# Softmax sums inverted in a compact layout, shared semaphores for emptied banks, and new numbers in the kernel's own planner

## The chip, the cores and the metric

One core of one Trainium2 chip runs the whole program. The time is device microseconds (us) for one execution. The core has five instruction streams: PE (TensorE, matmuls into PSUM), DVE (VectorE), ACT (ScalarE), POOL (GpSimd) and SP (SyncE, which here only issues DMAs). Each stream runs its instructions in the order in which they were written, and waits in front of an instruction until the semaphores it names have reached their values.

## The reference, cut to what matters

The input x is 4 batches of 1024 rows of 256 numbers in fp32. Three blocks follow one another, each with a residual:

```
x = x + 0.5 * ffn(layernorm(x))        # gate and up 256->704, silu(g) * u, down 704->256
x = x + attention(layernorm(x))        # 16 heads of 16, rotary positions, causal softmax
x = x + 0.5 * ffn(layernorm(x))        # the same weights again
```

The attention scores of a head are q.k / 4 with a causal mask; the softmax subtracts the maximum of the row, takes the exponential, and divides by the sum of the row. It is this division that the change touches.

## The kernel before, in words

**Stages.** The first feed-forward block works on 8 chunks of 512 rows (`ffn`, `x_pass`). Attention follows in 16 groups: 4 batches, and in each 4 groups of 4 heads (`NG = 4`, `GROUPS = 16`). The second feed-forward block is again 8 chunks. Products are formed from high and low parts in a rounded 32-bit format, so most matmuls come in threes.

**One group of attention** has two sweeps. The first (`maxima`, L861 and L871) computes the scores with queries on the partitions (piece `pe_s`), and DVE takes the maximum of each row from PSUM (`dve_max`, L1148). The maxima are gathered by DVE (`dve_nm`, L1157 to L1164), transposed by PE (L878), copied by ACT (L1015) and sent through a DRAM buffer (`nw`, L1343, and `nm`, L1350) into two extra rows of Q. The second sweep (`heads`) computes the scores transposed, shift included (`pe_st`, L892); ACT takes the exponential out of PSUM (`act_exp`, L1029); POOL zeroes the half above the diagonal (`pool_mask`, L1252); and PE multiplies with V (`pe_pv`, L909). V has 17 columns per head, the last one all ones, so row 17 of a head's result is the sum of its softmax. The first sweep of group n+1 runs beside the second sweep of group n. The projections for q, k and v of the next batch (L773) are laid between.

**The division.** For each group and each half of 512 queries (`c2`), ACT copies the result from PSUM to `OS` (`act_o`, L1037), SP writes it to DRAM (`ow`, L1356) and reads it back twice (`oc`): the 16 value rows of each head into `OC` (L1368), and the sum row broadcast to the same 16 partitions into `SC` (L1369). When two groups have filled the 128 partitions, DVE takes the reciprocal of the whole 128x512 tile `SC` in place (`dve_rc`, L1170), POOL multiplies (`pool_on`, L1258), ACT and POOL split the product into a high and a low part (L1042, L1263), and PE projects it (`pe_o`).

**The planner.** No order of work is written out by hand. `timetable()` lists all pieces with a place (a due time in us), a cost in ns, the pieces they come after, and the PSUM banks they need. `settle()` then plays the five streams forward: on an engine other than PE it takes the ready piece with the smallest place; on PE it takes the ready piece with the smallest cost-adjusted place that finds free banks and lies within `WINDOW` of the first piece not yet begun. `LAG` is the time that it adds from the end of a piece to its being visible elsewhere, `QUOTA` how many of the 8 banks the pieces `pe_s` and `pe_st` may hold, `MODE_PLACE` and `MODE_NS` what a change of matmul shape costs, `DMA_RATE` bytes per ns. The order and the banks that come out are what the streams are written from, so a wrong number in the planner costs no correctness, only a different order.

**Semaphores.** Each kind of piece has a semaphore of its own. Before a matmul writes into a bank, `take` waits for the pieces that emptied it. `wait_ge` leaves out a wait for a value that this engine has already met on the same semaphore.

The division in `heads`, as the planner sees it: `dve_rc` has the place `key + 6` and the cost `dve_ns(512)`, which is 65 + 512 / 0.96 = 598 ns.

Of the kernel before, what the change touches and what calls it, by code (L numbers as in the profile page):

```python
# [75 lines left out]

INNER = {"dve_va": ("dve_bn", "dve_ag"), "dve_nm": ("dve_mn", "dve_nh"), "pool_r": ("pool_ts", "pool_tc"), "dve_flagint": ("dve_flagsum",)}
# [31 lines left out]
LAG = {"PE": 165, "ACT": 130, "DVE": 90, "POOL": 80, "SP": 1900}  # L109
# [15 lines left out]
class Timetable:  # L125
# [21 lines left out]
    def settle(self):  # L147
# [30 lines left out]
        def choose(e):  # L178
# [23 lines left out]
        while todo or ends:  # L202
# [10 lines left out]
            for e in self.order:  # L213
                while free[e] <= now:
# [5 lines left out]
                    if e == "PE":  # L220
# [34 lines left out]
MODE_PLACE, MODE_NS, DMA_RATE, WINDOW = 2.0, 110, 250.0, 40.0  # L255
AHEAD = 4.0
QUOTA = {"pe_s": 4, "pe_st": 4}
# [37 lines left out]
def timetable():  # L295
# [18 lines left out]
    def x_pass(who, c, at):  # L314
# [7 lines left out]
        add(at + 2, 4 * 290, "act_xn", who, c, after=[("dve_nb", who, c)] + ([("pe_xT",) + xn + (1,)] if xn else []))  # L322
        for kt in range(2):
            add(at + 4, 436, "pe_xT", who, c, kt, after=[("act_xn", who, c), ("act_id",)] + (x_users(*x) if x else []), room=(1,))
# [26 lines left out]
    def ffn(ph, c, at):  # L351
        who, last = f"f{ph}", []
        for i in range(NI):
# [9 lines left out]
            if i < NI - 1:  # L363
                add(key, 908, "pe_g", ph, c, i, after=x_in(who, c) + w + room, room=(1,))
            add(key + 1, 908, "pe_u", ph, c, i, after=x_in(who, c) + w + room, room=(1,))
            gate = ("pe_g" if i < NI - 1 else "pe_u", ph, c, i)
            add(key + 1, act_ns(512) + 90, "act_silu", ph, c, i, after=[gate] + ([("dve_h",) + g] if g else []) + first,
# [3 lines left out]
            add(key + 2, act_ns(512), "act_hh", ph, c, i, after=[("dve_h", ph, c, i)] + room)  # L371
# [19 lines left out]
    def qkv(b, cc, at, z):  # L391
# [4 lines left out]
        for w in range(2):  # L396
            p.ring("T", 1, (b, cc, w))
            was = p.prior["T", (b, cc, w)]
            for ab in range(2):
                add(key(2 * w + ab), 1362, "pe_qk", b, cc, w, ab, after=x_in("a", c) + [("act_wh", "q"), ("pool_wl", "q")] + ([("pool_zl",) + was] if was else split), room=(1,))  # L400
# [30 lines left out]
    def maxima(gr, at, z):  # L431
# [3 lines left out]
        for c2 in range(2):  # L435
            drained = []
            for unit, n in zip(units, cost):
# [7 lines left out]
                add(key, mask + (2 if u == "a" else 1) * (wide * 0.443 + 12), "pe_s", *unit, after=[ld(gr, ch), ld(gr, c2), ("act_mk",)],  # L445
# [15 lines left out]
    def heads(gr, at, z):  # L461
# [4 lines left out]
        for unit, n in zip(units, cost):  # L466
# [5 lines left out]
            add(key, (2 if u == "a" else 1) * (max(512 - skip, 256) * 0.443 + 12), "pe_st", *unit,  # L472
# [6 lines left out]
            if u != 0:  # L479
# [6 lines left out]
                else:  # L486
                    w = sum({0: 1000, 128: 780, 256: 590, 384: 460}[e_skip(c2, i)] for i in (j - 1, j)) - 150
# [4 lines left out]
            if (j, u) == (4 * c2 + 3, "a"):  # L492
# [61 lines left out]
class Engine:  # L554
# [13 lines left out]
def macaron(nc, x_in, wgu, wd, wqkv, wo, gsc, usc, dsc, ident_in, cos_in, sin_in, mask_in, out):  # L568
    ctx = ExitStack()
    with ctx:  # L570
# [11 lines left out]
        def lay(at, *items):  # L582

            made = []
            for name, shape, dt in items:
# [15 lines left out]
        NH = place("NH", [P, 4])  # L601
        ONE = place("ONE", [P, 1])
        FL = place("FL", [P, 16])
        FS = place("FS", [1, 1])
        FLAG = place("FLAG", [1, 2], I32)
        ST, MV, VE, RS, NB = ([place(f"{n}{i}", [P, 4] + s) for i in range(2)]
                              for n, s in (("ST", [6]), ("MV", [2]), ("VE", []), ("RS", []), ("NB", [])))
        NP = [place(f"NP{i}", [P, 2, BT, 4]) for i in range(2)]
        NM = [place(f"NM{i}", [P, 2, 2, 2, 2, 4], F32R) for i in range(2)]
        NMT = [place(f"NMT{i}", [32, P], F32R) for i in range(2)]  # L610
        ONES = place("ONES", [2, 32], F32R)
# [55 lines left out]
        OD = nc.dram_tensor("od", (2, P, 512), F32, kind="Internal").ap()  # L667
        WGD = nc.dram_tensor("wgd", (2, P, 2, GUW), F32, kind="Internal").ap()
# [13 lines left out]
        for name in ("PE", "ACT", "DVE", "POOL", "SP"):  # L682
            for piece in plan.order[name]:
                for sem, by in raises(piece):
# [3 lines left out]
                    done[(sem,) + piece[1:]] = count[sem]  # L688
        pe, act, dve, pool, sp = (Engine(n, sems, done) for n in ("PE", "ACT", "DVE", "POOL", "SP"))
        S = sems  # L690
# [71 lines left out]
        def tensor_program(e, todo, general):  # L762
            tn = nc.tensor

            def take(piece):

                for was in emptied.get(piece, ()):
# [8 lines left out]
            for piece in todo:  # L776
# [24 lines left out]
                elif kind == "pe_flag":  # L801
# [3 lines left out]
                    tn.matmul(bank(*piece)[0:1, 0:6], ONE[:, 0:1], FL[:, 8:14], start=True, stop=True).then_inc(S["pe_flag"], 1)  # L805
# [238 lines left out]
        def vector_program(e):  # L1044
            ve = nc.vector
            for piece in plan.order["DVE"]:
                kind, a = piece[0], piece[1:]
                if kind == "dve_va":
# [15 lines left out]
                    ve.tensor_scalar(VE[k][:, :], MV[k][:, :, 1], EPS, None, ALU.add).then_inc(S["dve_va"], 1)  # L1064
                elif kind == "dve_nb":
# [3 lines left out]
                    ve.scalar_tensor_tensor(NB[k][:, :], MV[k][:, :, 0], -1.0, RS[k][:, :], ALU.mult, ALU.mult).then_inc(S["dve_nb"], 1)  # L1069
# [14 lines left out]
                elif kind == "dve_flagint":  # L1084
                    e.wait_ge("pe_flag")
                    ve.tensor_reduce(out=FS[0:1, 0:1], in_=bank("pe_flag")[0:1, 0:6], axis=AX, op=ALU.add).then_inc(S["dve_flagsum"], 1)
# [387 lines left out]
```

## Time and profile before

| | us |
|---|---|
| median of 3 runs | 982.24 |
| lowest and highest of the 3 | 974.79 and 982.36 |
| the profiled execution | 987.35 |
| its span, first to last instruction | 985.6 |

The profile is of one execution. Busy times are those of an engine's instructions; waits, branches and the issue of DMAs are not counted as busy. A PE weight load (PEld) overlaps the matmuls. The mean granted TensorE clock of the execution is 0.908 of full speed. Full speed is 2.4 GHz and the lower level, 0.50, is 1.2 GHz.

### The profile page before, as it was taken

How to read it: one execution, taken by the hardware profiler on the slowest of the kernel's cores; microseconds unless marked ns; L12 is line 12 of the kernel's file. 1: busy time of each engine (PE TensorE's matmuls, PEld its weight loads, DVE VectorE, ACT ScalarE, POOL GpSimd, SP SyncE). 2: the span in 40 equal slices, each digit the busy share in tenths (PEclk: the TensorE clock that was granted, in tenths of full speed). 3: DMA queues.
4: the chain of work that ended last, by engine and by line, in shares of the span. 5: the costliest groups of instructions: out<-in, count | busy, mean ns of one | idle time of the engine just before them, and what ended most of it. 6: DMA issues, size and time to landing. Idle time of an engine off the chain costs nothing.

```text
span 985.6 us, 17031 instructions
## 1 busy us (share of the span) xinstructions
PE 861.6 (87%) x6064; PEld 545.0 (55%) x6064; DVE 682.0 (69%) x1257; ACT 563.2 (57%) x1102; POOL 386.1 (39%) x361
## 2 busy tenths in 40 slices
PE   5699999969988989988898998798978878899996
PEld 4477888745544445644444464344434334777785
DVE  5575675868988779877787878777786742655442
ACT  5555665437465656664665655465635686465652
POOL 6556776352432234333134143221121322565453
PEclk9799999979996989986897988788979898999999
DMA  9500333035553325245054233431830110000101
GB/s 320 227 1 1 123 102 97 2 68 155 156 168 86 77 98 137 76 138 145 31 144 103 103 103 136 107 79 37 269 101 34 45 34 23 26 28 22 44 23 43
DMA packets 52320, 91.44 MB, mean 93 GB/s; under 512 B 6028, under 2 KB 17676, under 8 KB 51724
## 3 DMA queue, kind: packets, MB, share of 16 engines
q1 hardware_dynamic: 52092, 90.27, 30.2%
q8 instruction: 51, 0.84, 0.4%
q14 instruction: 33, 0.27, 0.1%
q10 hardware_dynamic: 144, 0.07, 0.0%
HBM read 47.49 MB, written 42.73 MB: 92 GB/s over the span
## 4 chain that ended last, share of the span: by engine, by line
PE 60%; DVE 15%; ACT 14%; issue 5%; DMA 2%; POOL 2%; SPq 1%; DVEq 0%; POOLq 0%; ACTq 0%
PE psum L909 12%; PE psum L799 12%; PE psum L773 10%; PE psum L861 9%; PE psum L892 7%; PE psum L824 7%; DVE NP L1148 7%; ACT PT L1029 5%; DVE SC L1170 3%; ACT XN L958 3%; PE psum L871 2%; ACT G_f L977 2%; DMA SC<-od 1%; ACT HH_f L987 1%; ACT XH L965 1%
## 5 line engine op out<-in xcount | busy, mean ns | idle before, releaser
L1148 DVE TENSOR_REDUCE NP<-psum 128x1 f32<-128x512 f32 (+3 forms) x640 | 364.3, 628 | 104.0 <-PE psum L871 74.3
L1029 ACT ACTIVATE PT<-psum 128x512 f32<-128x512 f32 (+2 forms) x640 | 307.9, 568 | 180.6 <-PE psum L892 179.5
L861 PE MATMUL psum<-K,Q 48*128 48x512 f32 (+2 forms) x768 | 159.8, 441 | 41.8 <-DVE NP L1148 31.7
L892 PE MATMUL psum<-Q,K 50*128 50x512 f32 (+2 forms) x768 | 153.8, 443 | 33.1 <-ACT PT L1029 18.0
L909 PE MATMUL psum<-PT,V 128*32 128x512 f32 (+3 forms) x1536 | 170.3, 568 | 0.4 <-ACT PT L1029 0.4
L1252 POOL TENSOR_SCALAR_AFFINE_SELECT PT<-PT 128x512 f32<-128x512 f32 x128 | 80.8, 638 | 206.1 <-ACT PT L1029 205.8
L799 PE MATMUL psum<-XH,WGH_f 128*128 128x512 f32 x352 | 147.2, 418 | 15.4 <-issue 6.7
L861 PEld LDWEIGHTS psum<-K,Q 48*128 48x128 f32 x768 | 77.1, 204 | 125.8 <-DVE NP L1148 48.5
L799 PE MATMUL psum<-XL,WGH_f 128*128 128x512 f32 x352 | 141.0, 401 | 0.0
L1209 POOL TENSOR_TENSOR HL_f<-HF_f,HH_f 128x512 fp32r<-128x512 f32 x80 | 103.0, 1294 | 94.1 <-ACT HH_f L987 93.8
L892 PEld LDWEIGHTS psum<-Q,K 50*128 50x128 f32 x768 | 77.4, 210 | 80.1 <-ACT PT L1029 31.8
L1099 DVE SCALAR_TENSOR_TENSOR HF_f<-psum,US,G_f 128x512 f32<-128x512 f32 x96 | 71.6, 750 | 58.8 <-ACT G_f L977 28.6
L824 PE MATMUL psum<-WDH_f,HH_f 128*128 128x256 f32 x384 | 90.0, 287 | 6.4 <-DVE HH_f L1106 5.6
L987 ACT ACTIVATE HH_f<-HF_f 128x512 fp32r<-128x512 f32 x96 | 60.4, 629 | 59.8 <-DVE HF_f L1099 59.0
L977 ACT ACTIVATE G_f<-psum,GS 128x512 f32<-128x512 f32 x96 | 64.8, 681 | 45.9 <-PE psum L799 45.1
L799 PEld LDWEIGHTS psum<-XH,WGH_f 128*128 128x128 f32 x352 | 67.8, 193 | 41.1 <-ACT G_f L977 9.3
L909 PEld LDWEIGHTS psum<-PT,V 128*32 128x32 f32 x1536 | 43.5, 118 | 78.7 <-issue 56.8
L824 PE MATMUL psum<-WDH_f,HL_f 128*128 128x256 f32 x320 | 78.9, 283 | 0.0
L824 PEld LDWEIGHTS psum<-WDH_f,HH_f 128*128 128x128 f32 x384 | 71.3, 193 | 11.4 <-issue 6.7
L799 PEld LDWEIGHTS psum<-XL,WGH_f 128*128 128x128 f32 x352 | 67.9, 193 | 12.8
L1258 POOL TENSOR_TENSOR OC<-OC,SC 128x512 f32<-128x512 f32 x16 | 20.3, 1270 | 131.5 <-DVE SC L1170 131.5
L824 PEld LDWEIGHTS psum<-WDH_f,HL_f 128*128 128x128 f32 x320 | 61.6, 192 | 0.4
(81 smaller groups left out, 1087.2 us busy)
## 6 DMA issues: line engine op xcount, KB each, us to landing
zd<-ZH SPq DMA_DIRECT2D x32, 512.0 KB, 3.8
Q<-zd SPq DMA_DIRECT2D x64, 192.0 KB, 3.7
K<-zd SPq DMA_DIRECT2D x64, 192.0 KB, 4.5
zd<-ZL SPq DMA_DIRECT2D x16, 512.0 KB, 4.6
od<-OS SPq DMA_DIRECT2D x32, 256.0 KB, 2.8
OC<-od SPq DMA_DIRECT2D x32, 128.0 KB
SC<-od SPq DMA_DIRECT2D x32, 128.0 KB
out<-X SPq DMA_DIRECT2D x16, 256.0 KB, 2.1
```

Of the source, the lines that this page charges most:

```text
L773: ins = tn.matmul(dst, x, w, start=(m == 0), stop=(m == len(terms) - 1))
L799: ins = tn.matmul(bank(*piece), w[ph][:, kt, col:col + P], x[k][:, kt, :], start=(n == 1), stop=(n == 6))
L824: ins = tn.matmul(dst, h[:, rows], w[ph][:, i, :], start=(n == 0), stop=(n == len(terms) - 1))
L861: ins = tn.matmul(dst, Q[k][r, p, t * P:(t + 1) * P], K[k][r, p, ch * 512:ch * 512 + w], start=(m == 0), stop=not diag)
L892: ins = tn.matmul(dst, K[k][r, p, j * P:(j + 1) * P], Q[k][r, p, 512 * c2 + base:512 * c2 + 512], start=True, stop=True)
L909: ins = tn.matmul(bank(*piece)[32 * h:32 * h + 32, skip:512], V[b % 2][:, col:col + 32], pt_view(gr, c2, j)[:, h, :], start=(j == 0), stop ...
L977: sc.activation(G[ph][slot[f"Gf{ph}", a]][ul, :], bank(*gate)[gl, :], ACT.Silu, scale=GS[gl, i:i + 1]).then_inc(S["act_silu"], 1)
L1029: sc.activation(dst, src, ACT.Exp, scale=0.25).then_inc(S["act_exp"], 1)
L1099: ve.scalar_tensor_tensor(HF[ph][k][ul, :], bank("pe_u", *a)[ul, :], US[ul, i:i + 1], G[ph][k][ul, :], ALU.mult, ALU.mult).then_inc(S["dve ...
L1148: ve.tensor_reduce(out=acc, in_=src, axis=AX, op=ALU.max, negate=True).then_inc(S["dve_max"], 1)
L1209: gp_.tensor_tensor(HL[ph][s][:, :], HF[ph][slot[f"Gf{ph}", a]][:, :], f32(HH[ph][s][:, :]), ALU.subtract).then_inc(S["pool_hl"], 1)
L1252: gp_.affine_select(out=pt, in_=pt, compare_op=ALU.is_ge, fill=0.0, base=0, pattern=[[0, 4], [1, P]], channel_multiplier=-1).then_inc(S["p ...
```

## The change

It has three parts.

1. **Division.** A new DMA `rs` reads the 4 x 512 sums of a group and half from DRAM into a compact tile `SU` of 128 partitions by 16; DVE takes the reciprocal of that tile into `RC`, once per group and half (32 times in place of 16); a new DMA `rw` writes it to a DRAM buffer `rd_`. The second read of `oc` now broadcasts the inverted sums from there. `pool_on` waits for the two `oc` of its groups and no longer for DVE.
2. **Semaphores.** The pieces of ACT that can empty a bank share one semaphore, `act_out`, and those of DVE another, `dve_out`. `take` goes through the emptying pieces from the highest value down, so that one wait per engine is left.
3. **The planner's numbers.** Lags, costs of pieces, the price of a change of shape and of a wait for two engines, a larger window (60 for 40), a quota of 5 banks for 4, and an urgency `URGE` by which `pe_s` and `pe_st` go ahead of other PE work while they hold few banks.

The small tiles of the layer norm are also placed differently in memory, with the same instructions on them.

```diff
-LAG = {"PE": 165, "ACT": 130, "DVE": 90, "POOL": 80, "SP": 1900}
+LAG = {"PE": 200, "ACT": 190, "DVE": 150, "POOL": 120, "SP": 1900}
...
-                cost = item[0] + (0 if self.mode[item[2]] == mode[0] else MODE_PLACE)
+                kind = item[2][0]
+                cost = item[0] + (0 if self.mode[item[2]] == mode[0] else MODE_PLACE) - URGE.get(kind, (0,) * 9)[held.get(kind, 0)]
...
-                            ns += MODE_NS
+                            ns += MODE_NS[mode[0], self.mode[piece]]
                             mode[0] = self.mode[piece]
+                        ns += WAIT_NS * (len({engine[x] for x in self.emptied.get(piece, ())}) - 1 > 0)
...
-MODE_PLACE, MODE_NS, DMA_RATE, WINDOW = 2.0, 110, 250.0, 40.0
+MODE_PLACE, WAIT_NS, DMA_RATE, WINDOW = 1.0, 80, 200.0, 60.0
+MODE_NS = {("full", "half"): 190, ("col", "half"): 110, ("half", "full"): 30, ("half", "col"): 30, ("full", "col"): 60, ("col", "full"): 60}
-QUOTA = {"pe_s": 4, "pe_st": 4}
+URGE = {"pe_s": (12, 12, 12, 12, 4, 0, 0), "pe_st": (12, 12, 8, 8, 0, 0, 0)}
+QUOTA = {"pe_s": 5, "pe_st": 5}
...
-                add(key, mask + (2 if u == "a" else 1) * (wide * 0.443 + 12), "pe_s", *unit, ...
+                add(key, mask + (2 if u == "a" else 1) * (wide * 0.443 + 40), "pe_s", *unit, ...
...
-                    w = sum({0: 1000, 128: 780, 256: 590, 384: 460}[e_skip(c2, i)] for i in (j - 1, j)) - 150
+                    w = sum({0: 790, 128: 600, 256: 420, 384: 250}[e_skip(c2, i)] for i in (j - 1, j))
...
+                add(key + 2.6, 600, *turn_of("rs", gr, c2), after=[turn_of("ow", gr, c2)])
+                add(key + 2.6, 280, "dve_rc", gr, c2, after=[turn_of("rs", gr, c2)] + ([turn_of("rw", *was)] if gr else []))
+                add(key + 2.6, 600, *turn_of("rw", gr, c2), after=[("dve_rc", gr, c2)] + ([turn_of("oc", *was)] if gr else []))
-                add(key + 2.5, 1200, *turn_of("oc", gr, c2), after=[turn_of("ow", gr, c2)] + free, size=2.6e5)
+                add(key + 2.6, 1200, *turn_of("oc", gr, c2), after=[turn_of("ow", gr, c2), turn_of("rw", gr, c2)] + free, size=2.6e5)
...
-                    add(key + 6, dve_ns(512), "dve_rc", b, gp, c2, after=[turn_of("oc", gr - 1, c2), turn_of("oc", gr, c2)])
-                    add(key + 6, pool_ns(512), "pool_on", b, gp, c2, after=[("dve_rc", b, gp, c2)])
+                    add(key + 6, pool_ns(512), "pool_on", b, gp, c2, after=[turn_of("oc", gr - 1, c2), turn_of("oc", gr, c2)])
...
     def wait_ge(self, sem, *step):
         value = self.done[(sem,) + step]
+        sem = EMPTIES.get(sem, sem)
...
-                for was in emptied.get(piece, ()):
+                for was in sorted(emptied.get(piece, ()), key=lambda was: -done[was]):
                     e.wait_ge(*was)
...
                 elif kind == "dve_rc":
-                    b, gp, c2 = a
-                    for g in range(2):
-                        e.wait_ge(*turn_of("oc", NG * b + 2 * gp + g, c2))
-                    n = 2 * (2 * gp + c2)
-                    ve.reciprocal(OC[n + 1][:, :], OC[n + 1][:, :]).then_inc(S["dve_rc"], 1)
+                    gr, c2 = a
+                    e.wait_ge(*turn_of("rs", gr, c2))
+                    if gr:
+                        e.wait_ge(*turn_of("rw", gr - 1, c2))
+                    ve.reciprocal(RC[c2][:, :], SU[c2][:, :]).then_inc(S["dve_rc"], 1)
...
+                elif name[:2] == "rs":
+                    gr, c2 = a
+                    e.wait_ge(*turn_of("ow", gr, c2))
+                    if gr:
+                        e.wait_ge("dve_rc", gr - 1, c2)
+                    src = OD[c2].rearrange("(h r) q -> h r q", h=4)[:, HD, :].rearrange("h (a n) -> h a n", n=16)
+                    sy.dma_start(SU[c2][:, :], src).then_inc(sem, 16)
+                elif name[:2] == "rw":
+                    gr, c2 = a
+                    e.wait_ge("dve_rc", gr, c2)
+                    if gr:
+                        e.wait_ge(*turn_of("oc", gr - 1, c2))
+                    sy.dma_start(RD_[c2].rearrange("h (a n) -> h a n", n=16), RC[c2][:, :]).then_inc(sem, 16)
...
-                    sy.dma_start(sc_[r, :], src[:, HD:HD + 1, :].broadcast_to([4, HD, 512])).then_inc(sem, 16)
+                    sy.dma_start(sc_[r, :], RD_[c2].unsqueeze(1).broadcast_to([4, HD, 512])).then_inc(sem, 16)
```

Other costs of pieces that change: the transposes of x 436 to 400 ns, the four normalising activations 1160 to 1964, gate and up 908 to 925, silu 567 to 586, the high part of the hidden tile 477 to 550, q and k projections 1362 to 1385.

## Rows read from the trace of the kernel before

**Rows 1.** The page, parts 1 and 2: busy time of each engine, and the granted clock.
```profile
PE 861.6 (87%) x6064; PEld 545.0 (55%) x6064; DVE 682.0 (69%) x1257; ACT 563.2 (57%) x1102; POOL 386.1 (39%) x361
PEclk9799999979996989986897988788979898999999
```

**Rows 2.** Windows by stage: length, busy of five engines, granted clock, DMA share, GB/s.
```profile
0.00:208.00 208.00, 179.33 (x1014) 145.06 (x1014) 137.50 (x290) 112.31 (x189) 121.30 (x96) 0.98 0.30 104
225.00:808.00 583.00, 514.89 (x4084) 271.24 (x4084) 457.44 (x815) 348.80 (x736) 168.51 (x186) 0.87 0.37 106
```

**Rows 3.** The chain that ended last: by line; first and last of ten stretches.
```profile
PE psum L909 12%; PE psum L799 12%; PE psum L773 10%; PE psum L861 9%; PE psum L892 7%; PE psum L824 7%; DVE NP L1148 7%; ACT PT L1029 5%; DVE SC L1170 3%; ACT XN L958 3%; PE psum L871 2%; ACT G_f L977 2%; DMA SC<-od 1%; ACT HH_f L987 1%; ACT XH L965 1%
...
312.53 3.26 DVE SC L1170
...
781.37 3.36 DVE SC L1170
```

**Rows 4.** Groups of instructions by line: busy, mean ns of one | idle before, releaser.
```profile
L1148 DVE TENSOR_REDUCE NP<-psum 128x1 f32<-128x512 f32 (+3 forms) x640 | 364.3, 628 | 104.0 <-PE psum L871 74.3
...
L1170 DVE RECIPROCAL SC<-SC 128x512 f32<-128x512 f32 x16 | 53.5, 3346 | 7.4 <-DMA SC<-od 7.4
...
L1162 DVE CAST NM<-NP 128x16 fp32r<-128x16 f32 x32 | 10.1, 316 | 1.0 <-DVE NP L1148 0.5
```

**Rows 5.** Timeline around one reciprocal: start, length, instruction, [idle before <-releaser].
```profile
357.06 3.35 DVE L1170 RECIPROCAL SC<-SC 128x512 f32<-128x512 f32 x1 [0.67 <-DMA SC<-od]
...
360.33 1.82 DVE L1148 TENSOR_REDUCE NP<-psum 128x1 f32<-128x512 f32 x3
...
361.60 0.80 PE L861 MATMUL psum<-K,Q 48*128 48x512 f32 x2 [3.20 <-DVE NP L1148]
```

**Rows 6.** Windows of 4 us, from 0.8 us after each of 16 reciprocals; one, and the sum.
```profile
357.90:361.90 4.00, 0.80 (x10) 0.29 (x2) 4.00 (x4) 0.11 (x1) 1.26 (x1) 0.82 0.97 358
...
sum 64.00, PE 29.20 PEld 13.94 DVE 61.38 ACT 24.82 POOL 27.20; mean PE 1.83 PEld 0.87 DVE 3.84 ACT 1.55 POOL 1.70
```

**Rows 7.** Windows of 14 us from the start of the 16 reciprocals: first, tenth, last.
```profile
289.10:303.10 14.00, 12.13 (x104) 6.68 (x105) 13.18 (x21) 9.04 (x21) 6.47 (x9) 0.73 0.88 234
...
636.00:650.00 14.00, 10.10 (x60) 4.14 (x60) 10.25 (x14) 6.68 (x14) 2.54 (x2) 0.60 0.05 20
...
842.00:856.00 14.00, 11.10 (x72) 9.42 (x71) 9.37 (x9) 6.02 (x10) 7.66 (x6) 1.00 0.01 1
```

**Rows 8.** Waits of PE in attention (225 to 808): total us, times, longest.
```profile
PE psum L861 <- DVE NP L1148: 31.7, 32, 3.6
PE psum L892 <- DVE NP L1148: 9.3, 8, 2.4
PE psum L892 <- ACT PT L1029: 9.1, 24, 0.9
...
PE psum L861 <- issue: 0.5, 2, 0.3
```

**Rows 9.** Waits around the division, whole span, and SP's longest wait.
```profile
POOL OC L1258 <- DVE SC L1170: 131.5, 16, 18.6
...
ACT OH L1042 <- POOL OC L1258: 32.3, 13, 4.3
...
DVE SC L1170 <- DMA SC<-od: 7.4, 5, 4.5
...
SPq L1343 <- ACT NMT L1015: 262.2, 28, 23.8
```

**Rows 10.** DMAs on the DRAM tensor of the division: issue and landing, min/median/max.
```profile
L1356 SPq DMA_DIRECT2D od<-OS x32: 319/344/1183, 227.5 to 834.4; - x32
...
DMA to landing us min/median/max: 2.0/2.8/15.3
```

**Rows 11.** The page, part 6: KB each, median us from issue to landing.
```profile
Q<-zd SPq DMA_DIRECT2D x64, 192.0 KB, 3.7
...
nmd<-NMT SPq DMA_DIRECT2D x32, 16.0 KB, 1.4
```

More of the change, by code:

```diff
@@ L363, in ffn @@
             if i < NI - 1:
-                add(key, 908, "pe_g", ph, c, i, after=x_in(who, c) + w + room, room=(1,))
-            add(key + 1, 908, "pe_u", ph, c, i, after=x_in(who, c) + w + room, room=(1,))
+                add(key, 925, "pe_g", ph, c, i, after=x_in(who, c) + w + room, room=(1,))
+            add(key + 1, 925, "pe_u", ph, c, i, after=x_in(who, c) + w + room, room=(1,))
             gate = ("pe_g" if i < NI - 1 else "pe_u", ph, c, i)
-            add(key + 1, act_ns(512) + 90, "act_silu", ph, c, i, after=[gate] + ([("dve_h",) + g] if g else []) + first,
+            add(key + 1, 586, "act_silu", ph, c, i, after=[gate] + ([("dve_h",) + g] if g else []) + first,
                 empties=[gate] if i < NI - 1 else [])
@@ L370, in ffn @@
                 empties=[("pe_u", ph, c, i)])
-            add(key + 2, act_ns(512), "act_hh", ph, c, i, after=[("dve_h", ph, c, i)] + room)
+            add(key + 2, 550, "act_hh", ph, c, i, after=[("dve_h", ph, c, i)] + room)
             add(key + 3, pool_ns(512) if i < NI - 1 else dve_ns(512), *hl_by(ph, c, i), after=[("act_hh", ph, c, i)])
@@ L399, in qkv @@
             for ab in range(2):
-                add(key(2 * w + ab), 1362, "pe_qk", b, cc, w, ab, after=x_in("a", c) + [("act_wh", "q"), ("pool_wl", "q")] + ([("pool_zl",) + was] if was else split), room=(1,))
+                add(key(2 * w + ab), 1385, "pe_qk", b, cc, w, ab, after=x_in("a", c) + [("act_wh", "q"), ("pool_wl", "q")] + ([("pool_zl",) + was] if was else split), room=(1,))
             banks_of = [("pe_qk", b, cc, w, ab) for ab in range(2)]
@@ L444, in maxima @@
                 mask = 0 if ch < c2 else (2 if u == "a" else 1) * 85
-                add(key, mask + (2 if u == "a" else 1) * (wide * 0.443 + 12), "pe_s", *unit, after=[ld(gr, ch), ld(gr, c2), ("act_mk",)],
+                add(key, mask + (2 if u == "a" else 1) * (wide * 0.443 + 40), "pe_s", *unit, after=[ld(gr, ch), ld(gr, c2), ("act_mk",)],
                     room=(2,), mode="half")
@@ L471, in heads @@
             was = pt_before(gr, c2, j)
-            add(key, (2 if u == "a" else 1) * (max(512 - skip, 256) * 0.443 + 12), "pe_st", *unit,
+            add(key, (2 if u == "a" else 1) * (max(512 - skip, 256) * 0.443 + 40), "pe_st", *unit,
                 after=([was] if was else ffn1_end) + [ld(gr, c2), ld(gr, j // 4), turn_of("nm", gr, c2), (f"dma_on{gr % QK}",)],
@@ L600, in macaron @@
         MB = place("MB", [P, P + 64], BF16)
-        NH = place("NH", [P, 4])
-        ONE = place("ONE", [P, 1])
+        CST = place("CST", [P, 8])
+        NH, ONE, FS = CST[:, 0:4], CST[:, 4:5], CST[0:1, 5:6]
         FL = place("FL", [P, 16])
-        FS = place("FS", [1, 1])
         FLAG = place("FLAG", [1, 2], I32)
-        ST, MV, VE, RS, NB = ([place(f"{n}{i}", [P, 4] + s) for i in range(2)]
-                              for n, s in (("ST", [6]), ("MV", [2]), ("VE", []), ("RS", []), ("NB", [])))
+        ST, MV = ([place(f"{n}{i}", [P, 4, s]) for i in range(2)] for n, s in (("ST", 6), ("MV", 2)))
+        ROW = place("ROW", [P, 2, 3, 4])
+        VE, RS, NB = ([ROW[:, i, n, :] for i in range(2)] for n in range(3))
         NP = [place(f"NP{i}", [P, 2, BT, 4]) for i in range(2)]
@@ L610, in macaron @@
         NMT = [place(f"NMT{i}", [32, P], F32R) for i in range(2)]
+        SU, RC = ([place(f"{n}{i}", [P, 16]) for i in range(2)] for n in ("SU", "RC"))
         ONES = place("ONES", [2, 32], F32R)
@@ L687, in macaron @@
                     count[sem] = count.get(sem, 0) + by
-                    done[(sem,) + piece[1:]] = count[sem]
+                    done[(signal,) + piece[1:]] = count[sem]
         pe, act, dve, pool, sp = (Engine(n, sems, done) for n in ("PE", "ACT", "DVE", "POOL", "SP"))
-        S = sems
+        S = sems | {signal: sems[sem] for signal, sem in EMPTIES.items() if sem in sems}
         def bank(*use):
@@ L804, in tensor_program @@
                     take(piece)
-                    tn.matmul(bank(*piece)[0:1, 0:6], ONE[:, 0:1], FL[:, 8:14], start=True, stop=True).then_inc(S["pe_flag"], 1)
+                    tn.matmul(bank(*piece)[0:1, 0:6], ONE, FL[:, 8:14], start=True, stop=True).then_inc(S["pe_flag"], 1)
                 elif kind == "pe_dn":
@@ L1085, in vector_program @@
                     e.wait_ge("pe_flag")
-                    ve.tensor_reduce(out=FS[0:1, 0:1], in_=bank("pe_flag")[0:1, 0:6], axis=AX, op=ALU.add).then_inc(S["dve_flagsum"], 1)
+                    ve.tensor_reduce(out=FS, in_=bank("pe_flag")[0:1, 0:6], axis=AX, op=ALU.add).then_inc(S["dve_flagsum"], 1)
                     e.wait_ge("dve_flagsum")
-                    ve.tensor_copy(FLAG[0:1, 0:1], FS[0:1, 0:1]).then_inc(S["dve_flagint"], 1)
+                    ve.tensor_copy(FLAG[0:1, 0:1], FS).then_inc(S["dve_flagint"], 1)
                 elif kind == "dve_h":
@@ L1255, in gpsimd_program @@
                     b, gp, c2 = a
-                    e.wait_ge("dve_rc", *a)
+                    for g in range(2):
+                        e.wait_ge(*turn_of("oc", NG * b + 2 * gp + g, c2))
                     n = 2 * (2 * gp + c2)
```

22 lines of the change are left out of this document (14 added, 8 removed).

## The prediction

> **What bounds the kernel now.** I read the page first. PE is busy 87% of the span and DVE 69%, and the row of granted clocks is full at both ends and ragged in the middle [rows 1]. The windows by stage say the same in numbers. The first feed-forward block runs at a clock of 0.98; attention, 225 to 808 us, takes 583 us at 0.87, with PE busy 514.9 us (88%) and DVE 457.4 us (78%) [rows 2]. So attention is where a change can gain. It has two losses. PE is idle for 583 - 514.9 = 68 us, and the clock below full costs 0.13 x 583 = 76 us, since PE at its lower level does half the work in the same busy time. PE's own waits there are on DVE emptying PSUM after the row maxima (31.7 + 9.3 us), and much less on ACT (9.1 us) [rows 8].
>
> DVE has long to do there (640 maxima of 628 ns), but one of its instructions is unlike the others: the reciprocal of a 128x512 tile, 16 times 3.35 us [rows 4]. The chain of waits that ended last goes through it ten times [rows 3]; the ten stretches add up to 31 us. The timeline around one shows how: DVE is shut for 3.35 us, no bank is emptied, and PE stands for 3.20 us until the maxima resume [rows 5]. The lower clock follows. In the 14 us from that start the clock is 0.76.
>
> **The change part by part.**
>
> *The old reciprocals go.* Take a window of 4 us from 0.8 us after each start, where PE has run out of banks: in the 16 windows PE is busy 29.2 of 64 us, 46% [rows 6]. At the 88% of the stage it would be 56.5 us. That is 27 us of PE time lost beside the 16 reciprocals, and I count it as regained. (The chain's 31 us is the same loss seen another way.)
>
> *The clock after them.* The 14 us from each start had clocks from 0.60 to 1.00 [rows 7], of which three stand there. For the 14 windows that lie in attention the mean is 0.74, a loss of 0.26 x 196 = 51 us of the stage's 76. The other 387 us of attention lose 25 us, 0.065 per us; at that rate the 196 us would have lost 13. So 38 us of clock loss goes with the reciprocals. Part of it has other causes close by (the window from 289 us is also one of heavy DMA traffic, 234 GB/s), and a PE that gets ahead meets its next wait sooner. I take half, 19 us; its bounds are 0 and 38.
>
> *The new reciprocals.* DVE has 32 on 128x16. The old instruction scaled by columns gives 3346 x 16 / 512 = 105 ns; the nearest row is another operation on 128x16, 316 ns [rows 4], and I take that: 32 x 0.316 = 10 us of DVE. What a us of DVE is worth comes from the old ones: (27 + 19) / 53.5 = 0.86. So -9 us (bounds -3 and -10).
>
> *The wait in front of them.* `dve_rc` now waits for `rs`, a DMA, which itself follows `ow`. Queued behind it on DVE are the row maxima, and for those PE waits. The old instruction waited 7.4 us in 16, its DMA having been due 3.5 us earlier than it (`key + 2.5` against `key + 6`) [rows 9]. At the same 0.46 us for each, 32 waits make 15 us; the old 7.4 go. Net 7.4 x 0.86 = -6 us. The lower bound is +6 (no waits left). The upper is the subject of a rival.
>
> *SP and the DMAs.* 64 DMAs more, about 8 KB each, with issues like the 344 ns of `od<-OS` [rows 10]: 22 us of SP's time in 583. SP spent 262 us in front of one line alone, waiting for ACT [rows 9], so it has room, and I cost it at nothing; without that room, `nm` and `ld` would come late by the round trip. The way from ACT's copy to `oc` grows by two hops. The small hop of the trace lands in 1.4 us and the loads of 192 KB in 3.7 [rows 11]; so 2 x (1.4 to 3.7) plus issue and reciprocal, 4 to 8 us, less the 3.35 that POOL's product no longer waits. It moves no end: PE has no row of waiting for the output projection, whose operands this is. The DMA traffic of attention fills 0.37 of the queues' time [rows 2]. The broadcast read is of the same size as before.
>
> The Trainium skill speaks against this part: "DMA: Bandwidth & Descriptors", in its rules for kernel authors, has it that transfers under 64 KB are mostly overhead, and its anatomy of one DMA gives a fixed cost of about 2 us, most of it the receipt of the write. By that, an estimate from that page of the skill, two hops add 4 us per group and half, 128 us in all, if each were waited out. The 16 KB row lands in 1.4 us, under the skill's figure, and nothing on PE waits for it, so I leave the sum as it is.
>
> *POOL and ACT behind the division.* POOL stood 131.5 us in front of `pool_on`, up to 18.6 us at once, and ACT 32.3 us in front of the high part that follows it [rows 9]. The planner booked the reciprocal at 598 ns where it took 3.35 us, so it placed both too early by 2.7 us: 12 x 2.7 = 32, which is ACT's row. With an honest cost they go. ACT has slack (349 of 583 us busy [rows 2]), so I count nothing here and keep it for the next term. Late next: `pool_on` behind the landing of `oc`, with the masks queued after it on POOL.
>
> *Semaphores.* They take waits out of PE's stream. The trace shows PE waiting for nothing but issue for 0.5 us in the whole stage [rows 8]. I take 0. From below it is 0, from above perhaps 5.
>
> *The new order.* What the planner will choose cannot be read off a trace. What it can win is bounded: 41 us of PE idling that is not beside reciprocals (68 - 27), 25 us of clock loss outside the windows and the 19 that I left inside: 85 us. The numbers move towards the rows (598 to 280 ns for a reciprocal that I put at 316). `URGE` and the fifth bank put the scores, which feed DVE and ACT, ahead of projections that nobody is in a hurry for, and DVE was idle for 104 us on the scores alone [rows 4]. Against it: fewer banks and later turns for `pe_pv`. I take about a fifth of the 85, 16 us, with -14 (the stage's 68 us of idling grow by a fifth) and 50 as ends. The feed-forward blocks I leave as they are: clock 0.98, and costs that moved by few per cent.
>
> **Sum.** 27 + 19 - 9 - 6 + 16 = 47 us. The profiled execution took 987.35 us (span 985.6), so it comes to 940 us. The median of the runs is 5 us under it, 982.24; I do not take off those 5, since three runs spread over 7.6 us. Forecast: **940 us**, 4.3% less than the median.
>
> **The rivals.** A measurement of this kernel can tell about 1% from no change: 972 to 992 is "the same".
>
> *A, everything goes.* No reciprocal and a good order leave a full clock: 27 + 38 + 6 - 3 + 30 and more, below 915, to about 890. For it: DVE would have 457 - 43 = 414 us to do and PE, at full clock, 515 - 76 = 439 in a stage of 583, so nothing forbids it. Against: the 25 us lost far from any reciprocal. Chance 0.12.
>
> *B, the gain turns into other waits.* With the reciprocal gone PE waits elsewhere: ACT and PT buffers, scores that take banks from `pe_pv`, weak clocks as before. Then only the 27 us remain, less 15 for the new DVE work and waits: 12, or 27 at best, and with a worse order (-14) nothing. 960 to 985, about half of it inside "the same". Chance 0.17.
>
> *C, slower: DVE waits out the round trip.* The place: `dve_rc`, 32 times, in front of the maxima. The price: a wait of w costs 0.86 w. The gains without this term are 53 us, so the kernel is no faster from w = 53 / (32 x 0.86) = 1.9 us, and slower by 10 us from 2.3 us. With w = 2.8, the median landing [rows 10], it is 77 us: 987 - 53 + 77 = 1011. For it: that DMA landed as late as 15.3 us once, the old wait was up to 4.5 us [rows 9, 10], and the place is now the same as the DMA's own. Against: the planner gives each DMA of these 2.5 us and more before DVE is sent there, longer than the 1.4 of the small hop, and the mean wait was 0.46 us with old numbers that were too quick. Chance 0.09.
>
> *D, the change does nothing.* For the semaphores that is what I expect. For the division it cannot be: the 3.35 us instructions are gone from the program. It has no chance of its own.
>
> **How the numbers follow.** The forecast has the remaining 0.62, on 915 to 965. With A all faster, and half of B, faster by over 1% has 0.62 + 0.12 + 0.07 = 0.81; the same 0.10; slower 0.09. The range is to leave out no more than 2 in 10: from 905, which takes in the upper part of A, to 975, which takes in the better half of B. Outside lie half of A, half of B's rest and C, together 0.2.
>
> **What would show it.** Right: DVE busy in attention down from 457 us by 40 to 50; small reciprocals near 0.3 us with short waits on the DMA; the chain without reciprocals; granted clock in attention at 0.92 or more in place of 0.87; PE's waits on the maxima (41 us) down by half; ACT's 32 us before the high part gone. Wrong: DVE waiting over 1 us per small reciprocal (C); PE waits that have moved to the exponentials at a clock of 0.87 (B); masks that wait on POOL behind `pool_on`, and P times V behind them; or feed-forward stages that changed their length by more than 5 us, of which I expect none.

## The result

The changed kernel takes 911.25 us (median of 4 runs, 907.12 to 914.58), the kernel before 981.78 us. The ratio is 0.9295 (95% interval 0.9237 to 0.9353): 7.1% faster. Ratios and intervals are made from the fast runs of each kernel. The forecast was 940 us with a range of 905 to 975, so the time lies inside, on the fast side: below the 915 to 965 that had the chance of 0.62, in the part that the range took over from rival A.

The page of the profile after, parts 1 and 2, answers to [rows 1]:

```profile
PE 825.9 (91%) x6066; PEld 532.8 (59%) x6066; DVE 635.8 (70%) x1273; ACT 559.8 (62%) x1102; POOL 387.6 (43%) x361
PEclk9899999989989799999999899999989789999999
```

The span went from 985.6 to 905.5 us. The same work keeps PE busy 36 us less (861.6 to 825.9), which is clock: the mean granted clock is 0.953 for 0.908. PE's idle time, span less busy, went from 124 to 80 us. So the 80 us are 44 us of standing and 36 us of running slowly. These are two single executions, the one before 5 us above its kernel's median and the one after the fastest of its four; by the medians the gain is 70.5 us. That the 36 us are clock can be checked: busy time times granted clock is nearly the same for both, 861.6 x 0.908 = 782 and 825.9 x 0.953 = 787.

Attention runs from the first to the last matmul with V, 222.8 to 832.8 us before and 217.6 to 755.5 after. The windows of the two, of the kernel before and then of the changed one (columns as in [rows 2]):

```profile
222.80:832.80 610.00, 536.72 (x4233) 280.44 (x4236) 464.78 (x830) 366.96 (x771) 176.97 (x195) 0.87 0.36 104
```

```profile
217.60:755.50 537.90, 499.53 (x4203) 261.03 (x4206) 418.32 (x834) 358.38 (x763) 175.65 (x193) 0.94 0.42 119
```

Attention gave 72 of the 80 us: 35 us of PE idling (73.3 to 38.4) and 37 us of PE busy time. DVE has 46 us less to do in it. The other 8 us lie in front of the first matmul with V (5.2) and behind the last one (2.8). The prediction named a change of more than 5 us there as a sign of being wrong, and the front just meets it. It is the passage from the feed-forward block into attention that got shorter, from 17.8 to 12.6 us (these windows of before and after); in the first 205 us PE is busy for 178.1 and 179.0 us.

```profile
205.00:222.80 17.80, 10.25 (x44) 6.68 (x42) 9.59 (x28) 7.95 (x15) 12.13 (x11) 0.71 0.45 101
```

```profile
205.00:217.60 12.60, 10.38 (x66) 8.27 (x65) 3.85 (x7) 7.95 (x15) 10.02 (x10) 0.86 0.60 125
```

The waits of the changed kernel around the division, in the whole span (total us, times, longest), answer to [rows 9], and those of PE from 220 to 755 us behind them to [rows 8]:

```profile
DVE NP L1163 <- PE psum L886: 57.5, 63, 9.7
POOL OC L1274 <- DMA SC<-rd_: 37.7, 11, 12.6
DVE RC L1185 <- DMA SU<-od: 22.2, 2, 13.0
ACT OH L1057 <- POOL OC L1274: 12.4, 5, 6.3
```

```profile
PE psum L907 <- ACT PT L1044: 11.4, 27, 1.0
...
PE psum L876 <- DVE NP L1163: 5.4, 16, 0.6
PE psum L907 <- DVE NP L1163: 2.8, 7, 0.6
```

PE's two waits on the row maxima fell from 41.0 to 8.2 us, and none is longer than 0.6 us where one was 3.6. The small reciprocal is one row among the groups (L1185), and its only waits on the DMA are two at the end, shown by the timeline:

```profile
L1185 DVE RECIPROCAL RC<-SU 128x16 f32<-128x16 f32 x32 | 7.6, 242 | 22.2 <-DMA SU<-od 22.2
```

```profile
736.09 0.25 DVE L1185 RECIPROCAL RC<-SU 128x16 f32<-128x16 f32 x1 [12.97 <-DMA SU<-od]
745.61 0.25 DVE L1185 RECIPROCAL RC<-SU 128x16 f32<-128x16 f32 x1 [9.27 <-DMA SU<-od]
```

By then the last row maximum is done (the last starts at 721.6 us), so DVE has no maximum to hold up, and from 736 to 760 us PE waits for ACT alone, 3.1 us: a large wait in the table that PE does not feel.

The chain of waits, by line, has no reciprocal left in its leading terms, and a DMA (`SC<-rd_`) in its place:

```profile
PE psum L814 13%; PE psum L924 12%; PE psum L788 11%; PE psum L839 9%; PE psum L876 8%; PE psum L907 8%; DVE NP L1163 7%; ACT PT L1044 5%; ACT XN L973 3%; DMA SC<-rd_ 3%; PE psum L886 2%; DVE HF_f L1114 2%; PE psum L799 1%; DVE ST L1072 1%; ACT XH L980 1%
```

### The profile page after: what moved, and what is told of

It is laid out like the page before. It is cut to its first block, busy times and chain, and to the rows that moved or that the text cites. A ratio compares the mean times of both kernels' runs of the same rounds, so it can differ in the third digit from the quotient of the medians.

```text
span 905.5 us, 16939 instructions
## 1 busy us (share of the span) xinstructions
PE 825.9 (91%) x6066; PEld 532.8 (59%) x6066; DVE 635.8 (70%) x1273; ACT 559.8 (62%) x1102; POOL 387.6 (43%) x361
## 4 chain that ended last, share of the span: by engine, by line
PE 65%; DVE 13%; ACT 11%; DMA 4%; issue 4%; POOL 1%; SPq 1%; DVEq 0%; POOLq 0%; ACTq 0%
PE psum L814 13%; PE psum L924 12%; PE psum L788 11%; PE psum L839 9%; PE psum L876 8%; PE psum L907 8%; DVE NP L1163 7%; ACT PT L1044 5%; ACT XN L973 3%; DMA SC<-rd_ 3%; PE psum L886 2%; DVE HF_f L1114 2%; PE psum L799 1%; DVE ST L1072 1%; ACT XH L980 1%
## 5 line engine op out<-in xcount | busy, mean ns | idle before, releaser
L907 PE MATMUL psum<-Q,K 50*128 50x512 f32 (+2 forms) x768 | 148.6, 425 | 18.6 <-ACT PT L1044 12.4
L876 PE MATMUL psum<-K,Q 48*128 48x512 f32 (+2 forms) x768 | 149.4, 418 | 15.6 <-ACT PT L1044 7.0
L924 PE MATMUL psum<-PT,V 128*32 128x512 f32 (+3 forms) x1536 | 155.3, 524 | 1.0 <-POOL PT L1267 1.0
L876 PEld LDWEIGHTS psum<-K,Q 48*128 48x128 f32 x768 | 72.4, 193 | 88.6 <-DVE NP L1163 43.2
L907 PEld LDWEIGHTS psum<-Q,K 50*128 50x128 f32 x768 | 71.4, 196 | 69.7 <-DVE NP L1163 27.2
L924 PEld LDWEIGHTS psum<-PT,V 128*32 128x32 f32 x1536 | 41.5, 113 | 74.5 <-issue 55.6
L886 PE MATMUL psum<-MB,EB 64*128 64x128 bf16 (+2 forms) x768 | 58.7, 229 | 0.0
```

The lines of the kernel that those rows point to most:

```text
L876: ins = tn.matmul(dst, Q[k][r, p, t * P:(t + 1) * P], K[k][r, p, ch * 512:ch * 512 + w], start=(m == 0), stop=not diag)
L886: ins = tn.matmul(dst, EB[r, half, :], m, start=False, stop=(half == 1))
L907: ins = tn.matmul(dst, K[k][r, p, j * P:(j + 1) * P], Q[k][r, p, 512 * c2 + base:512 * c2 + 512], start=True, stop=True)
L924: ins = tn.matmul(bank(*piece)[32 * h:32 * h + 32, skip:512], V[b % 2][:, col:col + 32], pt_view(gr, c2, j)[:, h, :], start=(j == 0), stop ...
```

## The experiments

Theory 1: the block of 3.35 us on DVE stopped PE and cost it its clock, and the new order adds a smaller part of its own. Rival 2: the planner's numbers did it. Rival 3: the division did it all. Ratios are to the kernel before as timed beside each run, with their 95% intervals. A cost or gain "by the ratios" is a difference of two ratios times 982 us; each is uncertain by some 7 to 9 us.

**The three parts, each alone.** `d_only` has the new division with its four places in the plan, `p_only` the planner's numbers and rules, `s_only` the shared semaphores:

```diff
# d_only: dve_rc on 128x16, DMAs rs and rw, oc reads rd_; also the small tiles of the layer norm where the changed kernel has them
# p_only: LAG, MODE_PLACE, MODE_NS, WAIT_NS, DMA_RATE, URGE, QUOTA, WINDOW, costs of pieces; nothing else
# s_only: EMPTIES, and take() from the highest value down; nothing else
```

> The kernel before with the new division alone; planner numbers and semaphores are the old ones. Theory 1 (the blocks of 3.35 us carried the loss, the prediction's terms): 27 + 19 - 9 - 6 = 31 us gained, about 950 us, PE waits on the row maxima in attention down from 41 us to under 20, clock there 0.90 to 0.92. Rival 2 (the planner's numbers carried it, the division is a small part): at most 10 us gained, 972 or more, waits and clock as before. Rival 3 (the division carried all 70 us): 910 to 920.

> The kernel before with the new planner numbers alone; the reciprocal stays 128x512 and is still booked at 598 ns. Theory 1: the prediction gave the order 16 us, 966 us; since the whole change gave 70 us and the division's terms make 31, up to 39 us, 943. Rival 2: 60 us or more, 920. Rival 3: nothing, 980, since a better order cannot help while DVE is shut for 3.35 us sixteen times.

> The kernel before with the shared semaphores alone; the order of work is the same. Theory: PE waited for nothing but issue for 0.5 us in attention, so 982 us, within 0.5%. Rival: each wait less in PE's stream saves its issue of some 0.05 us, and a few hundred of them make 10 to 20 us, 965 to 970.

Measured: `d_only` 944.59 us, 0.9658 (0.9608 to 0.9707). `p_only` 965.34 us, 0.9845 (0.9801 to 0.989). `s_only` 983.68 us, 1.0038 (1.0012 to 1.0064). Theory 1 has both numbers: 34 us for the division, where its terms made 31, and 15 us for the order, where the term was 16. Rivals 2 and 3 fall. In `d_only` PE's waits on the maxima (whole span) are down from 41 to 18 us, and the clock of attention is 0.92:

```profile
PE psum L865 <- DVE NP L1152: 12.2, 26, 1.4
...
PE psum L896 <- DVE NP L1152: 5.7, 8, 1.8
```

The order of work moved with the division: by the planner's lists, 523 of PE's 1154 pieces stand at another place than before. So the 34 us are the division with the plan that it brings, and the fall of the waits alone does not show what the blocks cost (the booking below).

But 0.9658 x 0.9845 is 0.951, and the whole gave 0.9295. Some 20 us came only when the parts met.

**The semaphores in the new order.**

> The changed kernel with one semaphore per kind of piece, as before; division and planner numbers are the new ones. Division alone gave 0.966 and the numbers alone 0.985, together 0.951 if they multiply, 934 us; the whole gave 0.9295, 913. Theory 1 (division and order help each other): this kernel has all of it, 913 us, within 0.5% of the changed one. Rival (the missing 20 us are the semaphores', which only tell when the fifth bank and the new order make two waits per matmul common): 930 us or more.

Measured: 917.67 us, 0.9349 (0.9313 to 0.9386). Against 0.9295 (0.9237 to 0.9353) that is half a per cent, and the intervals overlap. The order of work is that of the changed kernel, piece for piece. The semaphores are not the missing 20 us; whether they are worth 5 us in this order and nothing in the old one stays open.

**An honest booking, in the old and in the new order.** The old reciprocal was booked at 598 ns:

```diff
-                    add(key + 6, dve_ns(512), "dve_rc", ...
+                    add(key + 6, 3350, "dve_rc", ...
```

`h_only` is the kernel before with this line; `no_d_h` is the changed kernel with the old division and this line.

> The kernel before with one number changed: the planner books the 128x512 reciprocal at 3350 ns and no longer at 598. Theory 1 (the block itself costs): the stall of PE stays, at most 10 us gained, 972 to 982, though ACT's 32 us before the high part shrink. Rival (the block was only misplaced; a planner that knows of it lays other work beside it): 20 us or more gained, 960 or less.

> The changed kernel with the old 128x512 reciprocal, honestly booked at 3350 ns. Theory 1 (the block of 3.35 us stops PE whatever the order): 960 us, near the kernel with new numbers alone, and PE waits on the maxima of 30 us or more. Rival (what was worth 20 us beyond the two parts is an honest plan, which the new kernel has because its reciprocal is small and rightly booked): 940 or less.

Measured: `h_only` 987.09 us, 1.004 (1.0003 to 1.0077). `no_d_h` 947.92 us, 0.9605 (0.9531 to 0.9678). In the old order the booking is worth nothing. ACT's wait behind the product went as foreseen, from 32.3 to 3.2 us. PE's waits on the maxima went too, from 41.0 to 16.7 us, with all sixteen blocks still there; but PE then waited on the exponentials for 30.3 us (18.0 before). These waits of `h_only`, and the busy line of its page (the profiled execution, of 991.2 us, is its longest):

```profile
PE psum L892 <- ACT PT L1029: 30.3, 54, 3.6
PE psum L861 <- DVE NP L1148: 14.6, 32, 1.1
...
ACT OH L1042 <- POOL OC L1258: 3.2, 3, 1.5
...
PE psum L892 <- DVE NP L1148: 2.1, 5, 0.8
```

```profile
PE 877.2 (89%) x6064; PEld 543.5 (55%) x6064; DVE 685.4 (69%) x1257; ACT 562.5 (57%) x1102; POOL 386.3 (39%) x361
```

So a low wait on the maxima is no proof that the blocks are gone, and `d_only`'s 18 us are no more than an honest booking gives. Next to `h_only`, where the order is as honest, `d_only` has PE idle for 102 us in place of 112 and busy for 839 in place of 877: in this pair the division pays by the clock (0.943 for 0.900) more than by standing less. By the ratios it is 38 us there (1.004 to 0.9658).

In the new order it is different: 0.9605 against the 0.9845 of `p_only`, whose reciprocal is still booked at 598 ns (`no_d_h` also has the semaphores, worth half a per cent at most, and the small tiles of the layer norm at their new places, which no run has alone). Here are most of the missing 20 us. The new numbers are worth about 15 us on a plan that is wrong by 2.75 us at sixteen places, and about 36 on one that is right there (`d_only` to the changed kernel; 43 from `h_only` to `no_d_h`; both with the semaphores). The new division brings the right booking with it. And the step from the honest old division to the new one, 0.9605 to 0.9295, is 3.2% with the small tiles the same on both sides, near the division alone in the old order (3.4%, or 3.8% from `h_only`). I expected 960 us here, and waits on the maxima of 30 us or more; the time came out between the two theories and the waits at 17.3 us, so that part of theory 1 failed, and the rival's mechanism is real. These waits of `no_d_h`, and its busy line:

```profile
PE psum L872 <- DVE NP L1159: 11.7, 28, 0.8
...
PE psum L903 <- DVE NP L1159: 5.6, 9, 2.9
```

```profile
PE 851.6 (90%) x6066; PEld 540.2 (57%) x6066; DVE 682.9 (72%) x1257; ACT 564.3 (60%) x1102; POOL 386.4 (41%) x361
```

**Rules or costs.** `no_urge` keeps the new costs and lags and takes back the rules; `rules_old_costs` does the reverse (with a flat `MODE_NS` of 110 and no `WAIT_NS`):

```diff
# no_urge
-URGE = {"pe_s": (12, 12, 12, 12, 4, 0, 0), "pe_st": (12, 12, 8, 8, 0, 0, 0)}
-QUOTA = {"pe_s": 5, "pe_st": 5}
+URGE = {}
+QUOTA = {"pe_s": 4, "pe_st": 4}      # and WINDOW 60.0 -> 40.0
```

> The changed kernel with its measured costs and lags, but without the urgency, with a quota of 4 banks and a window of 40. Theory 1 (the rules of choice feed DVE and ACT, and the costs only follow the trace): 930 us, most of the order's gain gone. Rival (the costs carry it): 915 us.

> The changed kernel with the new rules of choice (urgency, quota of 5, window of 60), but with the old costs of pieces, lags, price of a change of shape and data rate. Costs without rules gave 955. Theory 1 (the rules carry the order's gain, and the costs carry nothing): 910 to 925. Rival (the rules only work on a plan that is true to the trace): 935 or more.

Measured: `no_urge` 955.15 us, 0.9738 (0.9693 to 0.9783), which is 8 us by the ratios slower than `d_only` with its old costs (their intervals just touch, and `no_urge` has the semaphores too). `rules_old_costs` 928.82 us, 0.9475 (0.942 to 0.9529), between the two expectations. By the ratios the rules are worth 43 us where the costs are new and 18 where they are old. The costs are worth 18 us where the rules are in force, and cost 8 where they are not. Neither theory of the two runs has this: each part needs the other. Without the rules PE waits longest on the maxima and the exponentials again, these of `no_urge`:

```profile
PE psum L907 <- ACT PT L1044: 21.8, 37, 3.9
PE psum L876 <- DVE NP L1163: 19.0, 34, 2.1
```

The urgency, the quota and the window were not taken apart.

**DVE waiting for the sums, on purpose.**

```diff
-                        end = dma_free + LAG[e]
+                        end = dma_free + (0 if piece[0][:6] == "dma_rs" else LAG[e])
```

> The changed kernel, but the planner takes the sums' DMA as landed the moment it is issued, so DVE is sent to each of the 32 small reciprocals some 1.9 us early and must wait for the DMA in front of the row maxima. This is the prediction's slower rival on purpose. By its price (0.86 us per us of wait) 32 waits of 1.5 to 1.9 us cost 41 to 52 us: 955 to 965 us. Rival (DVE has slack of some 20% and the banks filled ahead cover a wait under 2 us, as they did not cover 3.35): 10 us or less, 913 to 923.

Measured: 940.27 us, 0.9555 (0.9499 to 0.961), 26 us above the changed kernel by the ratio, and between the two expectations. But the waits are few and short: eight between 300 and 650 us, together 7.6 us, the longest of them 1.72, and four longer ones after 700 us, the last three of them (5.1 to 8.6 us) where the maxima have run out. One of the eight:

```profile
459.82 0.25 DVE L1185 RECIPROCAL RC<-SU 128x16 f32<-128x16 f32 x1 [1.72 <-DMA SU<-od]
```

At 0.86 per us they explain 7 us of the 26. To see whether the rest is only another draw of the order, `nudge` touches the plan without changing anything real:

```diff
-                add(key + 2.6, 280, "dve_rc", *...
+                add(key + 2.6, 242, "dve_rc", *...
```

> The changed kernel with the planner's cost of the small reciprocal at its measured 242 ns in place of 280. Nothing real changes but the order of work in the details. Theory (differences of 10 us between plans mean something): 913 us, within 5. Rival (any touch of the plan moves the time by 10 us or more, so the 27 us that the early reciprocals cost are not their 8 us of waits but another draw of the order): 10 us or more away from 913.

Measured: 915.02 us, 0.9322 (0.9276 to 0.9367), which its interval can't tell from 0.9295. This one touch moved the time by 3 us by the ratio, 4 by the medians. It is not a small one in the plan: played through, it puts 233 of PE's 1154 pieces at other places, and the early booking 377. So this draw of the order was harmless; one draw does not say how far others spread, and what the other 20 us of `early_rc` are is not settled. To move the reciprocals forward in DVE's stream alone is no way out: on the planner's lists, two places for all of them are enough to close a circle. DVE would stand before sums whose P times V is queued, on PE, behind scores that need the banks of the maxima behind the reciprocal. No run has it.

**The block by itself.** The last two keep every order of the changed kernel and give DVE useless work, 54.6 us in sixteen pieces of 3.4 us, or 59.1 us in 49 pieces of 1.2 us. The planner knows of neither:

```diff
# block, behind the small reciprocal of every odd group
+                    for n in range(3 * (gr % 2)):
+                        ve.tensor_reduce(out=FL[:, (6, 7, 14)[n]:(6, 7, 14)[n] + 1], in_=COS[:, :], axis=AX, op=ALU.max)
# spread, the same instruction behind every 13th row maximum
+                    if maxima % 13 == 6:
```

> The changed kernel, every order the same, with three more DVE instructions behind every second small reciprocal: maxima over 1024 constant columns into a scratch column nobody reads, about 1.1 us each, so DVE is shut for 3.4 us in one piece, 16 times, as the old reciprocal shut it. Theory 1 (the block itself is what was removed, 0.86 us of time per us): 54 x 0.86 = 46 us more than the changed kernel, 957, the clock loss up with it. Rival (the old cost came from the place the block had in the old order; the new order keeps banks filled and covers it): under 15 us more, 925 or less.

> The changed kernel, every order the same, with the same kind and nearly the same sum of extra DVE work (49 maxima over 1024 constant columns of 1.1 us, 54 us in all), but one at a time, behind every 13th of the 640 row maxima. Theory 1 (what stops PE is a block longer than the filled banks last): under 20 us more than the changed kernel, 915 to 931. Rival (DVE's work is what counts, in whatever pieces, because DVE is all but a bound beside PE): the same as the kernel with the blocks in one piece, some 957.

Measured: `block` 967.12 us, 0.9845 (0.9789 to 0.9901); `spread` 953.66 us, 0.9684 (0.962 to 0.9747). First three views of `block` (the group of the added instruction, the busy line of the page, PE's waits on the maxima), then the same three of `spread`:

```profile
L1187 DVE TENSOR_REDUCE FL<-COS 128x1 f32<-128x1024 f32 x48 | 54.6, 1192 | 0.1
```

```profile
PE 854.0 (88%) x6066; PEld 544.7 (56%) x6066; DVE 692.5 (72%) x1321; ACT 562.5 (58%) x1102; POOL 387.2 (40%) x361
```

```profile
PE psum L907 <- DVE NP L1163: 19.9, 15, 3.1
PE psum L876 <- DVE NP L1163: 16.8, 20, 3.9
```

```profile
L1168 DVE TENSOR_REDUCE FL<-COS 128x1 f32<-128x1024 f32 x49 | 59.1, 1207 | 0.0
```

```profile
PE 854.8 (90%) x6066; PEld 540.1 (57%) x6066; DVE 691.1 (72%) x1322; ACT 562.0 (59%) x1102; POOL 387.0 (41%) x361
```

```profile
PE psum L876 <- DVE NP L1164: 16.2, 34, 1.6
PE psum L907 <- DVE NP L1164: 12.5, 21, 2.4
```

The blocks alone bring back most of the 70 us: 54.6 us of DVE cost 54 us by the ratios (56 by the medians; 46 were expected), 1.0 per us. PE stands in front of the maxima for 36.7 us again, up to 3.9 at once, and the clock falls from 0.953 to 0.919. In the timeline of `block` one stall is like the old one of [rows 5], only shorter:

```profile
361.10 3.41 DVE L1187 TENSOR_REDUCE FL<-COS 128x1 f32<-128x1024 f32 x3
...
365.15 0.61 PE L876 MATMUL psum<-K,Q 48*128 48x384 f32 x2 [1.84 <-DVE NP L1163]
```

But `spread` was expected below 931 and came to 954, where its rival has it (957): 59.1 us of DVE in short pieces cost 38 us by the ratios (42 by the medians), 0.65 to 0.72 per us. So most of the price is DVE's work as such. Theory 1 as I put it (only a block longer than the filled banks hurts) falls.

The other third is not shown to be the length of the piece. `no_d_h` has sixteen blocks of 3.35 us too, but booked: against the changed kernel its DVE is busy 47 us more (682.9 for 635.8) and costs 30 us by the ratios, 0.65 per us, no more than the short pieces. And `block`, unbooked, has the ratio of `p_only`, whose blocks are unbooked as well, 0.9845 both. So a block that the planner knows costs no more here, within the uncertainty of 9 us, than scattered work; what raises the price to 1.0 may be its length, its place or its missing booking, and no run takes these apart (an unbooked and a booked block at the same place would). The two ways of losing show in PE's line of `block` and `spread`. Idle (966.5 - 854.0 = 112 us for `block`, 953.4 - 854.8 = 99 us for `spread`, 80 without either) rises by 33 and 19 us, busy by 28 and 29. The slower clock is paid in full in both cases, the standing much more for the block.

## Why the prediction came out as it did

*The mechanism was right in the main.* DVE's busy time fell by 46 us (40 to 50 foretold), the clock of attention rose to 0.94 (0.92 or more), PE's waits on the maxima fell to a fifth (half), and the reciprocal left the chain. `d_only` measured the division with its clock at 34 us against 31 in the sum, and from `no_d_h` to the changed kernel it is 30. Two signs came out otherwise: ACT's wait before the high part fell from 32.3 to 12.4 us and is not gone, and the front end changed by 5.2 us. The waits on the maxima proved a poor sign, since a booking alone lowers them as much (`h_only`).

*The terms of the division, one by one.* The small reciprocal takes 242 ns, not 316: 7.6 us of DVE for the 10 in the sum. Its wait on the DMA was put at 15 us and is 0 inside attention: the planner sends DVE late enough. With these two at their measured sizes the sum is 27 + 19 - 7 + 6 = 45 for a measured 34. So the 31 came near 34 by two errors that cancel: the regained standing and clock (46) were about 10 us too high, and the wait 15 us. The price of a us of DVE, 0.86, is above the 0.73 of `d_only` (34 us for 46 us of DVE) and lies between the 0.65 to 0.72 of work spread out or booked and the 1.0 of an unbooked block.

*Slips in the working.* The clock was charged on the length of a stretch, idle time included, where PE can lose by it only while it is busy. Over its busy time attention loses 0.13 x 515 = 67 us and not 76, and the 14 windows of [rows 7], each with its own clock, 41 and not 51. Busy time times clock bears this out: attention holds 536.7 x 0.87 = 467 us of full-clock work before and 499.5 x 0.94 = 470 after. With it the clock's 38 us become 30 (41 less the 11 that these windows would have lost at the rate of the rest) and their half 15, which takes 4 of the 10 us off. Two of the sixteen 4 us windows [rows 6] lie behind 808 us, so 44 us and not 41 of the stage's idling are away from reciprocals. And in 12 x 2.7 = 32 the 12 has no source: ACT waited 13 times, for 16 reciprocals. That the booking made this wait is shown by `h_only` all the same.

*The order was the mis-sized term.* It stood at 16 us and is worth 15 alone, but 36 in company (0.9658 to 0.9295, of which the semaphores may be a few). Of the 29 us between 940 and 911 these are about 20; 3 are the division, and 5 that the sum started from the profiled execution, 987, and not from the median, 982. What I missed stood in two sentences of mine that I did not join: the planner booked the reciprocal at 598 ns where it took 3350, and the planner's new numbers move towards the trace. I counted the first as ACT's idle time and the second as a gain of its own. `no_d_h` shows that the second depends on the first.

*The semaphores* were put at 0 with 5 as the upper end: +0.4% in the old order and -0.5% in the new one (the latter within the intervals).

*The rivals, and luck.* A (everything goes, below 915) is what the time says, 911, with 0.12 given to it; the main forecast, 915 to 965, missed it, and that the range held is owed to the half of A that it took in. Its mechanism is half there: attention's clock is 0.94 and not full, and PE still idles 38 us. C did not come: SP had room (its 64 new DMAs took 29 us to issue, at medians of 571 and 326 ns, for the 22 of the prediction), and stood in front of `rw` for DVE rather than DVE for it:

```profile
SPq L1385 <- DVE RC L1185: 99.7, 27, 9.4
```

The hops did move something: `pool_on` waits 37.7 us for its DMA (131.5 for DVE before), and the chain has it with 3%, about where the reciprocal stood. `rd_<-RC` lands in 1.4 us (median), like the small hop before [rows 11].

## What to carry to other kernels

An elementwise instruction whose operand is a broadcast can be done before the broadcast; look for it on the engine that empties PSUM, and count what it frees at about 0.65 to 0.75 us of time for each us in this kernel, up to 1.0 where it is a block that the plan does not know, although that engine is idle a fifth of the stage. Where a planner writes the order, one cost that is wrong by 2.75 us can hide more than half of what better numbers would bring (15 us for 36), so the expensive rare instruction is to be booked as the trace has it first. New costs without new rules made it worse by some 8 us: the parts of such a change have to be timed together too. A row of waits that shrinks is not yet a gain: with the booking alone it shrank by 24 us, and the time did not move.

## What was not expected of the hardware

The reciprocal takes 3346 ns for 512 columns of fp32 where other DVE instructions on the same shape take 680 to 750 ns, and 242 ns for 16 columns: between these two sizes about 6.3 ns for each further column.

A mean can mislead for short instructions. The cast of 128x16 that served as the nearest row in the prediction (316 ns on average) has a median of 182 ns in both kernels, and in the changed one single ones of up to 2.05 us (the line's own view: min/median/max):

```profile
L1177 DVE CAST NM<-NP x32: 168/182/2052, 158.9 to 722.6; 128x16 fp32r<-128x16 f32 x32
```

What makes the few long ones was not looked into.
